# Router logits from the first normalised tile and the output projection; the statistics of x from accumulating passes of ScalarE

## What is computed

```
def _layernorm(x, eps=1e-05):
    m = jnp.mean(x, axis=-1, keepdims=True); v = jnp.var(x, axis=-1, keepdims=True)
    return (x - m) / jnp.sqrt(v + eps)
...
    x = x + _L0_xattn_ref(_layernorm(x), ctx_1024, Wq, bq, Wk, bk, Wv, bv, Wo, bo)   # batch by batch, softmax(q k / 4) v, then Wo
    x = x + _L0_ffn_ref(_layernorm(x), router_w, router_b, weights1, bias1, weights2, bias2)
...
    # _L0_ffn_ref
    logits = x_flat @ router_w.T + router_b
    routed_idx = jnp.argmax(logits, axis=-1)
    # expert e: relu(relu(x @ w1[e] + b1[e]) @ w2[e] + b2[e]), 64 hidden units; each token takes its own expert's
```

## Time and profile before

| | |
|---|---|
| median of 3 runs | 1223.89 us (1223.77 to 1226.08) |
| profiled execution, its own time | 1223.15 us |
| its span | 1221.3 us |
| busy over the span | TensorE 1097.5 (90%), VectorE 925.0 (76%), ScalarE 858.5 (70%), GpSimd 847.3 (69%) |
| granted clock, mean | 0.972 |
| attention part, about | up to 965 us |
| page table to the end | from 999.46 us |

### The profile page before, as it was taken

The page is one execution under the profiler, slowest core; times in us unless marked ns, Lnnn a source line. Parts: engine busy times, 40 slices in busy tenths (PEclk is TensorE's granted clock), DMA queues, the critical chain, the costliest instruction groups (busy, mean ns, idle before and its releaser), DMA issues.

```text
span 1221.3 us, 39225 instructions
## 1 busy us (share of the span) xinstructions
PE 1097.5 (90%) x15399; PEld 845.1 (69%) x15399; DVE 925.0 (76%) x2321; ACT 858.5 (70%) x2020; POOL 847.3 (69%) x1613
## 2 busy tenths in 40 slices
PE   5999999999999999999999999999998419998893
PEld 4777777777777777777777777777776319977772
DVE  4787888888888888888888888888877427866772
ACT  4777777777777777777777777777776306655551
POOL 4544777677777777777777777777764656777776
PEclk9999999999999999999999999999999859999997
DMA  7415222522222222222222222222110136676650
GB/s 243 147 56 121 71 72 71 142 80 76 76 73 79 82 83 75 80 71 72 72 78 74 72 71 72 71 72 72 59 41 29 52 132 205 198 215 205 205 161 17
DMA packets 91156, 120.40 MB, mean 99 GB/s; under 512 B 14096, under 2 KB 73883, under 8 KB 90781
## 3 DMA queue, kind: packets, MB, share of 16 engines
q1 hardware_dynamic: 77150, 84.04, 24.2%
q0 software_dynamic: 13824, 33.85, 7.7%
HBM read 60.61 MB, written 59.31 MB: 98 GB/s over the span
## 4 chain that ended last, share of the span: by engine, by line
PE 60%; DVE 20%; POOL 7%; DMA 5%; issue 4%; ACT 3%; SPq 1%; POOLq 0%; DVEq 0%; ACTq 0%
PE pB L832 10%; PE pA L774 9%; PE pB L824 8%; PE sc L782 7%; DVE mx L595 6%; PE sc L806 5%; POOL out L419 4%; PE sc L765 4%; PE sc L815 3%; ACT arena L468 3%; DVE nrm L621 3%; PE m L791 3%; PE sc L1000 3%; DMA out<-arena 2%; PE m L798 2%
## 5 line engine op out<-in xcount | busy, mean ns | idle before, releaser
L595 DVE TENSOR_REDUCE mx<-m 128x4 bf16<-128x512 f32 x512 | 322.6, 670 | 10.7 <-PE m L791 10.5
L468 ACT ACTIVATE arena<-sc 128x512 f32<-128x512 f32 x512 | 264.5, 603 | 47.5 <-PE sc L815 47.5
L419 POOL DMA_INDIRECT out<-arena x160 | 157.0, 981 | 60.9 <-issue 31.1
L615 DVE STREAM_TRANSPOSE tr<-pB 128x512 f32<-128x512 f32 x128 | 91.8, 717 | 106.3 <-PE pB L824 106.3
L806 PE MATMUL sc<-qk 32*128 32x256 f32 x2048 | 167.0, 397 | 0.5 <-DVE rbp L674 0.5
L824 PE MATMUL pB<-arena 128*32 128x128 f32 x4096 | 159.8, 276 | 1.5 <-issue 1.0
L386 POOL DMA_INDIRECT pages<-row,slot_i x128 | 130.4, 1019 | 40.0 <-issue 37.0
L832 PE MATMUL pB<-wo_s,aT 128*128 128x256 f32 x512 | 138.0, 392 | 8.7 <-DVE aT L626 8.7
L824 PEld LDWEIGHTS pB<-arena 128*32 128x32 f32 x4096 | 99.0, 109 | 44.6 <-issue 43.6
L774 PE MATMUL pA<-cHi,wqkv 128*128 128x512 f32 x252 | 119.0, 474 | 9.4 <-DVE wqkv L660 9.4
L774 PE MATMUL pA<-xnT,wqkv 128*128 128x512 f32 x372 | 124.7, 443 | 0.0
(11 more groups left out here) (141 smaller groups left out, 2714.9 us busy)
## 6 DMA issues: line engine op xcount, KB each, us to landing
arena<-pages SPq DMA_DIRECT2D x160, 130.0 KB
cT<-ctxT SPq DMA_DIRECT2D x64, 256.0 KB, 3.8
xs<-x_in SPq DMA_DIRECT2D x128, 128.0 KB, 3.3
pages<-empty SPq DMA_DIRECT2D x120, 130.0 KB, 3.1
pages<-empty SPq DMA_DIRECT2D x1, 5200.0 KB, 19.8
out<-arena POOLq DMA_INDIRECT x160
w2s<-w SPq DMA_DIRECT2D x1, 2080.0 KB
qk<-w SPq DMA_DIRECT2D x1, 2064.0 KB, 8.2
```

What stands on the lines that cost most here:

```text
L419: pool.indirect_dma_start(out_rows, bass.IndirectOffsetOnAxis(pr[:, r, COL_TOKEN:COL_TOKEN + 1].bitcast(U32), 0), pr[:, r, 0:D], None, bou ...
L468: act.activation(pt[:, u % 2, g].rearrange("p i k -> p (i k)"), sc[g][:, :], ACT.Exp).then_inc(S["exp_out"], 1)
L595: ins = dve.tensor_reduce(mx[:, 32 * g:32 * g + 4], mb[i][:, :].rearrange("p (h k) -> p h k", h=4), AX.X, ALU.max)
L615: dve.transpose(tr[:, :], pB[:, :]).then_inc(S["tr_out"], 1)
```

## The change

The second normalised tile, its transposes and the products of it with the router's weights are no longer made. As a sum before the layer norm's scaling, a token's logit is (x + attention output) times the centred router weights `wr_s`. The part of x comes from the first norm's transposed tile: `logits(s+1)` from `xnTf` (a float32 copy of the transposes, a new first half of `xnT_copy`), transposed, and multiplied by the standard deviation of the first norm into 32 more columns of `xs` (`x_logits`). The part of the attention output comes from 32 more columns of `wo_s`, the product of output and router weights made at the start, so that `project_out`, `residual` and `add_bo` work on D + E = 288 columns for 256. `best` then scales by the second norm's 1/std and adds the router's bias. Setup steps for these weights are added in step -1 (`mean_router`, `output_bias`, `router_weights`, `router_bias` on TensorE, with partners on VectorE; `router_weights` also makes the logits of chunk 0 and waits for each copy in between). The router's chain runs one chunk nearer to the scores (`best(s-1)` in place of `best(s-2)`, and so on), places of `choose`, `scan` and `slot_sum` on VectorE move ahead of `attended`, and GpSimd's order becomes another.

The sums of x and of its squares for the first norm come from `stats1` on ScalarE (one `Copy` and one `Square` with accumulator for each batch) in place of `bn_stats` and `bn_aggr` on VectorE; `rstd1` has seven operations for four. In `row` the four extra columns stand first. The context's loads are asked for at other points, and one wait of SyncE goes.

```diff
-COL_TOKEN, COL_EXPERT, COL_MEAN, COL_RSTD = 256, 257, 258, 259
+COL_TOKEN, COL_EXPERT, COL_MEAN, COL_RSTD, X0 = 0, 1, 2, 3, 4
...
-        wo_s = sb("wo_s", [2, D])
+        wo_s, won_s = sb("wo_s", [2, D + E]), sb("won_s", [2, D])
+        mean_w, shift_e = sb("mean_w", [P]), sb("shift_e", [2])
...
-        xs = sb("xs", [4, QB, D])
-        row = sb("row", [4, QB, ROW])
-        xn, xn2 = sb("xn", [QB, D]), sb("xn2", [QB, D])
+        xs = sb("xs", [4, QB, D + E])
+        row = sb("row", [4, QB, X0 + D + E])
+        xn, junk, junk_x = sb("xn", [QB, D]), sb("junk", [2, D]), sb("junk_x", [2, D])
         xnT = sb("xnT", [2, 2, QB * P], F32R)
-        xn2T = sb("xn2T", [2, QB * P])
+        xnTf = sb("xnTf", [2, QB * P])
...
-            sp.dma_start(wo_s[:, :, :], wo).then_inc(S["ld_wo"], 16)
+            sp.dma_start(wr_s[:, :, :], wr).then_inc(S["ld_wr"], 16)
+            sp.dma_start(wo_s[:, :, 0:D], wo).then_inc(S["ld_wo"], 16)
             for u in range(QB):
                 load_x(1, u)
-            sp.dma_start(wr_s[:, :, :], wr).then_inc(S["ld_wr"], 16)
...
-                    if u == 3 and q >= 2:
-                        after(sp, "scattered", 64, q - 2, 63)
...
-                    if u == 3 and live(q + 4):
-                        load_ctx(q + 4, 0)
-                    if u == 0 and q >= 1 and live(q + 3):
-                        load_ctx(q + 3, 1)
+                    if u in (1, 2) and live(q + 3):
+                        load_ctx(q + 3, u - 1)
...
             def rstd1(q):
-                r, m, g = rs1[:, q % 2, :], nm1[:, q % 2, :], ag1[:, q % 2]
-                after(pool, "agg1_out", 4, q, 3)
+                r, m, v = rs1[:, q % 2, :], nm1[:, q % 2, :], vr1[:, q % 2, :]
+                after(pool, "stat1_out", 4, q, 3)
                 if q >= 2:
                     after(pool, "xn_out", 2, q - 2, 1)
-                pool.tensor_scalar(r, g[:, :, 1], EPS, None, ALU.add).then_inc(S["var1_out"], 1)
+                    after(pool, "lg_out", 1, q - 2, 0)
+                pool.tensor_scalar(sx1[:, q % 2, :], sx1[:, q % 2, :], -1.0 / D, None, ALU.mult).then_inc(S["mean1_out"], 1)
+                pool.tensor_scalar(sq1[:, q % 2, :], sq1[:, q % 2, :], EPS, None, ALU.add).then_inc(S["eps1_out"], 1)
+                after(pool, "mean1_out", 1, q, 0)
+                pool.tensor_tensor(mm1[:, :], sx1[:, q % 2, :], sx1[:, q % 2, :], ALU.mult).then_inc(S["mm1_out"], 1)
+                after(pool, "eps1_out", 1, q, 0)
+                after(pool, "mm1_out", 1, q, 0)
+                pool.tensor_tensor(v, sq1[:, q % 2, :], mm1[:, :], ALU.subtract).then_inc(S["var1_out"], 1)
                 after(pool, "var1_out", 1, q, 0)
-                pool.tensor_tensor(r, r, half[:, :], ALU.pow).then_inc(S["pow1_out"], 1)
+                pool.tensor_tensor(r, v, half[:, :], ALU.pow).then_inc(S["pow1_out"], 1)
                 after(pool, "pow1_out", 1, q, 0)
-                pool.tensor_tensor(m, g[:, :, 0], r, ALU.mult).then_inc(S["mr1_out"], 1)
-                after(pool, "mr1_out", 1, q, 0)
-                pool.tensor_scalar(m, m, -1.0, None, ALU.mult).then_inc(S["rstd1_out"], 1)
-
-            def rstd2(q, h):
...
+            def rstd2(q):
+                r, m = row[:, q % 4, :, COL_RSTD], row[:, q % 4, :, COL_MEAN]
+                after(pool, "sq_out", 4, q, 3)
...
                 after(pool, "xn_out", 2, q, 1)
-                pool.tensor_tensor(xs[:, q % 4], xs[:, q % 4], bo_s[:, :].unsqueeze(1).to_broadcast([P, QB, D]),
+                after(pool, "lg_out", 1, q, 0)
+                pool.tensor_tensor(xs[:, q % 4], xs[:, q % 4], bo_s[:, :].unsqueeze(1).to_broadcast([P, QB, D + E]),
                                    ALU.add).then_inc(S["xb_out"], 1)
...
             split(0)
             rstd1(0)
             split(1)
-            for s in range(-1, NQ + 3):
+            rstd1(1)
+            for s in range(-1, NQ + 2):
+                if live(s - 2):
+                    slots_as_integers(s - 2)
+                    scatter(s - 2)
                 if live(s - 1):
-                    rstd2(s - 1, 0)
-                if live(s - 3):
-                    place(s - 3)
-                if live(s + 2):
-                    rstd1(s + 2)
+                    rstd2(s - 1)
                 if s >= 0 and live(s + 2):
                     split(s + 2)
-                if live(s - 3):
-                    slots_as_integers(s - 3)
                 if live(s + 1):
                     add_bo(s + 1)
-                if live(s - 3):
-                    if live(s - 1):
-                        after(pool, "sq_out", 4, s - 1, 3)
-                    scatter(s - 3)
                 if live(s - 1):
-                    rstd2(s - 1, 1)
-                if live(s - 2):
-                    meta(s - 2)
-                    fresh_pages(s - 2)
+                    meta(s - 1)
+                if live(s + 3):
+                    rstd1(s + 3)
+                if live(s - 1):
+                    fresh_pages(s - 1)
+                    place(s - 1)
...
+            def stats1(q, u):
+                act.wait_ge(S[f"ld_x{q % 4}_{u}"], q // 4 * 16 + 16)
+                if q >= 2:
+                    after(act, "rstd1_out", 1, q - 2, 0)
+                if q * QB + u >= 1:
+                    act.wait_ge(S["stat1_out"], q * QB + u)
+                act.activation(junk_x[:, 0], xs[:, q % 4, u, 0:D], ACT.Copy, accum_out=sx1[:, q % 2, u:u + 1]).then_inc(S["sumx_out"], 1)
+                act.activation(junk_x[:, 1], xs[:, q % 4, u, 0:D], ACT.Square, scale=D ** -0.5,
+                               accum_out=sq1[:, q % 2, u:u + 1]).then_inc(S["stat1_out"], 1)
+
             act.wait_ge(S["ld_wk"], 16)
             act.activation(wqkv[:, 1, 0], wraw[:, 1], ACT.Copy).then_inc(S["wk_hi"], 1)
+            for u in range(QB):
+                stats1(0, u)
...
-                act.activation(xnT[:, 0, :, 2 * P * h:2 * P * (h + 1)], xnT_bank(q, h)[:, :].rearrange("p (c t) -> p c t", c=2),
+                if q >= 1:
+                    after(act, "xnTl_out", 2, q - 1, h)
+                act.activation(xnTf[:, :, at], xnT_bank(q, h)[:, :].rearrange("p (c t) -> p c t", c=2), ACT.Copy).then_inc(S["xnTf_out"], 1)
+                after(act, "xnTf_out", 2, q, h)
+                act.activation(xnT[:, 0, :, at], xnTf[:, :, at], ACT.Copy).then_inc(S["xnT_out"], 1)
...
-                    if u == 0 and live(s - 2):
-                        if s == 2:
-                            act.wait_ge(S["rbp_out"], 1)
-                        logits_copy(s - 2)
+                    if u == 1 and s >= 0 and live(s + 1):
+                        logits_copy(s + 1)
                     if live(s):
                         exps(s, u)
                     if u == 3 and live(s + 2):
                         xnT_copy(s + 2, 0)
                     if u == 0 and live(s + 1):
                         xnT_copy(s + 1, 1)
-                    if u == 1 and live(s - 1):
-                        xn2T_copy(s - 1, 0)
-                    if u == 3 and live(s - 1):
-                        xn2T_copy(s - 1, 1)
                     if live(s + 1):
                         v_copy(s + 1, u)
-                    if u == 0 and live(s - 2):
-                        logits_across(s - 2)
-                    if u == 2 and live(s - 2):
-                        rank_copy(s - 2)
+                    if s == -1 and u == 2:
+                        logits_copy(0)
+                    if u == 2 and live(s - 1):
+                        rank_copy(s - 1)
                     if s == -2 and u == 2:
                         for v in range(QB):
                             norm1(0, v)
                     if s >= 0 and live(s + 2):
                         for v in normal_rows(s, u):
                             norm1(s + 2, v)
-                    if u in (0, 2) and live(s - 1):
-                        norm2(s - 1, u)
-                        norm2(s - 1, u + 1)
                     if live(q1):
                         squares(q1, u1)
+                    if s >= 0 and live(s + 3):
+                        for v in ((0,), (1,), (2, 3), ())[u]:
+                            stats1(s + 3, v)
                     if live(q):
                         if q == 0 and n == 2:
                             act.wait_ge(S["mask_ready"], 1)
                     if s == -1:
                         for v in normal_rows(s, u):
                             norm1(1, v)
+                        stats1(2, u)
...
+            def x_logits(q):
+                after(dve, "lgT_done", 1, q, 0)
+                after(dve, "std1_out", 1, q, 0)
+                if q >= 4:
+                    after(dve, "x2_out", 4, q - 4, 3)
+                dve.tensor_tensor(xs[:, q % 4, :, D:D + E], sc[3][:, 0:P].rearrange("p (u e) -> p u e", e=E),
+                                  sd1[:, q % 2, :].unsqueeze(2).to_broadcast([P, QB, E]), ALU.mult).then_inc(S["lg_out"], 1)
+
             def best(q):
```

(75 more changed lines are left out.)

228 lines of the change are left out of this document (116 added, 112 removed).

## The result

The changed kernel takes 1385.71 us (median of 4 runs, 1384.26 to 1387.24), the kernel before, run beside it, 1224.93 (4 runs, 1223.77 to 1226.08): a ratio of 1.1313, 95% interval 1.1293 to 1.1332. It is slower by 13%. The profiled execution took 1386.37 us (span 1384.5), 163.2 more than that of before. Mean granted clock 0.956; busy over the span TensorE 1122.5 us (81%), VectorE 961.1, ScalarE 905.0, GpSimd 840.8.

What follows compares the result with a forecast made beforehand. TensorE was taken to set the pace, so its waits count. 28 steps x (0.56+1.8+2.2) = 128, other four steps +7, start +10, end -13, clock 17: +149 on 1223.15 gives 1372 us, range 1275 to 1425.

Steps and rivals of the forecast that it cites:

- the three stalls: Waits from late ScalarE statistics, the scan in pass 3 and the VectorE-GpSimd port: +0.56, +1.8 and +2.2 us a step.
- statistics behind the squares: ScalarE: statistics between squares and `mxT_copy`, two batches in pass 2, make `mxT_copy` late: +0.56 us a step.
- scan in pass 3: VectorE's scan waits for `fresh`, queued on GpSimd behind `rstd1`, so the projection comes late: +1.8 us a step.
- port, `best` against `add_bo`: Pass 1: VectorE's two-input operations of `best` wait for GpSimd's SBUF-reading `add_bo`: +2.2 us a step.
- clock: TensorE's long waits lower its granted clock: 0 to 1.15 us a step, half taken, 28 x 0.6 = 17 us.
- the other four steps: Steps 0, 29, 30 and 31 get only parts of the change: +3, +2, +1 and +1, together +7 us.
- start: Eight batches of statistics before `norm1(0)` and the router-weight chain in step -1: +10 us, bounds 6 and 14.
- end: From last residual to expert loads, only the last chunk's router work remains: 21 us for 34.7, so -13.
- (a): Rival: no collision of `best` with `add_bo`, no long wait, no clock loss: 1291 us; chance 0.17.
- (b): Rival: only ScalarE is late; `fresh_out` comes in time and nothing collides: 1241 us; chance 0.08.
- (c): Rival: faster, as the statistics hide on ScalarE and `rstd1` is early too: 28.3 a step, 1193 us; chance 0.08.
- (d): Rival: all stalls and a clock drop for each long wait, two a step: 1420 us; chance 0.07.

Runs made afterwards that it cites:

- e3: The changed kernel with both GpSimd moves, `add_bo` behind `meta` and a wait for `nrm`, `fresh_pages` ahead of `rstd1`: 1236.3 us, ratio 1.01.
- e1: The changed kernel with `add_bo` moved on GpSimd's queue behind `meta` and a wait for VectorE's product `nrm` of pass 2: 1321.62 us, ratio 1.0795.
- e2: The changed kernel with `fresh_pages` ahead of `rstd1` on GpSimd's queue: 1328.33 us, ratio 1.0856.
- e5: e3 with the statistics ahead of the squares on ScalarE: 1196.91 us, ratio 0.977.
- e6: e1 plus an extra GpSimd `memset` that only writes, in `add_bo`'s old place: 1323.46 us, ratio 1.0808.
- e7: The changed kernel with the statistics back on VectorE, so the router part alone: 1341.95 us, ratio 1.0957.
- e4: e3 with one batch of statistics in each pass, in place of one, one, two and none: 1405.1 us, ratio 1.1477.
- e10: e4 with `place` ahead of `rstd1` on GpSimd's queue: 1283.85 us, ratio 1.0485.

## Why the prediction was right, step by step

The direction, the three stalls and the range held: 1385.71 lies 14 over the 1372 and inside 1275 to 1425, and the forecast is the case that happened. Its terms, over steps 1 to 28 where a step is meant (sum before 819.7, after 978.6):

| term | predicted | measured |
|---|---|---|
| statistics behind the squares | +0.56 a step, 16 | +0.59, 836.3 - 819.7 = 16.6 (e3) |
| scan in pass 3 | +1.8, 50 | 31.96 - 29.87 = 2.09, 59 (e1 against e3) |
| port, `best` against `add_bo` | +2.2, 62 | 32.14 - 29.87 = 2.27, 64 (e2 against e3) |
| clock | 17 | 978.6 - 28 x 34.29 = 18.5 |
| the other four steps | +7 | +8.8 |
| start | +10 | 40.78 - 30.92 = 9.9 |
| end | -13 | 19.7 - 34.7 = -15.0 |
| expert part | 0 | 222.4 - 221.8 = 0.6 |
| sum | 149 | 163 |

**Statistics.** M3 was to be M2+8.5 and is M2+8.46; a batch followed by another costs 1.01 (616.73 to 617.74) for the 0.97, the last 0.81 for 0.84. One detail was wrong: pass 0 was not TensorE's own 7.13 but 7.29, because its one batch of statistics also stands ahead of the key copies; with the batch moved away (e5) it is 7.11. The other passes, each up to 0.05 shorter than predicted, made up for most of it.

**Scan.** `rstd1` starts at M2+6.99 (predicted 6.9), `fresh` ends at M2+10.60 (10.6). The size is off by 0.3: the scan took 0.47 where I had given it the 0.3 of the small operations, and the pass grew a little more than the projection's delay. Over 28 steps that is 8 of the 14 us missing.

**Port.** I expected the first product to be held, for 2.2 to 2.6 us, and gave as a bound that `add_bo` slips between the two. The bound is what the shown step and 21 others of steps 1 to 28 have: the first product starts 0.06 to 0.19 before `add_bo` and is nearly free, the second pays 2.3. In six steps, the first and five that follow a step with slow passes, it is the first (about 2.5 us). A tenth of a microsecond decided which, so that the place of the collision was forecast, and the order in it was not. The sum per step, 2.2, is as predicted. e1 takes `add_bo` away and the wait with it, and e6 shows that the reading is what counts.

**Clock.** One drop in some steps was predicted at 0.6 a step on average; it came as 2.7 us in seven steps of 28 (granted clock 0.83 and 0.84 over passes 2 and 3 of step 8, between the two levels of 1.2 and 2.4 GHz, and 1.00 in step 16), 18.5 in all. That the sum came out near is luck: neither the price of a drop nor the number of steps was what I had taken. The 1.15 was also read from a stretch that ends too soon: in the kernel before the clock is 0.50 over 938 to 940 us, the lower level, and still 0.89 on average over 940 to 945, another 0.55 us.

**Ends.** Both within 2 us of what was worked out, the start in part by luck: up to the first M the granted clock was 0.87 in the changed kernel and 0.94 in the one before, and e1, e2 and e3, with the same start and 1.00, have their first M at 38.7 to 39.5, that is +7.8 to 8.6. The chain behind the last residual is 19.7 for the 21.

**The rivals.** (a), no collision, is e1: 1322 with 27 us of clock loss, which it had left out, so 1295 without for its 1291; (b), ScalarE late alone, is e3: 1236 for its 1241. (c), faster, named the right condition, that the statistics hide on ScalarE: e5 meets it by their place in ScalarE's queue, with both moves on GpSimd's, at 1197 for its 1193. (d) fell: passes 2 and 3 were both slow in seven steps of 28, not in each.

**Not settled.** The stalls add up (2.09 + 2.27 = 4.36 for the 4.42 that both cost together), but the clock doesn't: its loss is 18.5 us in the changed kernel, 27 in e1 (921.9 - 28 x 31.96), which waits less, 21 in e2, 24 in e7 and none in e3. So e1 and e2 gained 64 and 57 us for stalls of 65 and 60 in steps 1 to 28 and some in the last steps, and both together 149. Which pattern of waits brings the drop was not found.

## What to carry to other kernels

Work moved to an idle engine costs by its place in that engine's queue: the same eight activations, two for each batch, cost 1.45 us a step more behind the squares (29.87) than ahead of them (28.42), where the engine was waiting anyway. When a step of an in-order queue gets a new and later event to wait for, list what stands behind it and who waits for that; here that was `fresh_pages`, and in e4, once more, `place`. Large GpSimd operations that read SBUF should be held by a semaphore to a place where VectorE has no two-input operation on its critical chain, since a shift of the queue can put another one there, as in e10.
